# Last dense-expert stage: the product on GpSimd, the turned gates copied by VectorE

## The chip, the cores and the metric

The kernel runs on one core of one Trainium2 chip. Its time is the device time of one execution in microseconds. The core has engines with a queue each, which take their instructions in order and wait for each other by semaphores: TensorE (PE, matmuls; PEld is its loading of weights), VectorE (DVE), ScalarE (ACT), GpSimd (POOL) and SyncE (SP, which issues transfers).

## The reference

A stack of six layers works on x of 2 x 2048 x 256 values in f32, that is 4096 tokens of 256 features. The last layer, a mixture of 8 small experts of which each token uses two, is the one that the change touches:

```python
def _L1_ffn_ref(x, router_w, w1, w2, w3):
    expert_scores = x_flat @ router_w.T
    top_scores, selected = jax.lax.top_k(expert_scores, TOPK)
    top_scores = jax.nn.softmax(top_scores.astype(jnp.float32), axis=-1)
    ...
    x1 = jax.lax.ragged_dot(xb, w1b, gs)
    x3 = jax.lax.ragged_dot(xb, w3b, gs)
    h = jax.nn.silu(x1) * x3
    routed = jax.lax.ragged_dot(h, w2b, gs).astype(x.dtype)
    weighted = routed * scores_sorted[:, None]
...
x = x + 0.5 * _L0_ffn_ref(_layernorm(x, axis=-1), ...)
x = x + _L0_attn_ref(_layernorm(x, axis=-1), ...)
x = x + 0.5 * _L0_ffn_ref(_layernorm(x, axis=-1), ...)
x = x + 0.5 * _L1_ffn_ref(_layernorm(x, axis=-1), ...)
x = x + _L1_attn_ref(_layernorm(x, axis=-1), ...)
x = x + 0.5 * _L1_ffn_ref(_layernorm(x, axis=-1), ...)
```

## The kernel before

x stays in SBUF through all layers. The two `_L1_ffn_ref` layers are computed densely by `ffn1`: every token goes through all 8 experts (8 x 64 = 512 hidden features, `H1`), and a gate per token and expert, zero for six of eight, is multiplied in. `ffn1` is called twice: as ffn1a, where `combine` is given (it also sums the tables that the layer before left in HBM), and as ffn1b, the last stage of the kernel, where `combine` is None and `x_out` is given. The mixing layer (`attn1`) lies between them.

Tokens come in 8 blocks of 512 (`NB`), hidden features in 4 chunks of 128 (`NM1`, index m). For a block and chunk, TensorE makes two projections in PSUM: `ps_a` (named main_ps_k in the trace) and `ps_b` (`up`, line 2291). ScalarE writes `silu` from the one and `b16` from the other (`keep_ab`, lines 2226 and 2228). VectorE multiplies the two to `prod` (`hidden` with part 0, line 2162). The gates of a block, 16 rows of 512, are turned by TensorE into `ps_g`, copied into `gate_t`, and spread over the 128 features of chunk m by one matmul into `ps_c` (`spread`, line 2300). VectorE multiplies `prod` with `ps_c` to `h` (`hidden` with part 1, line 2167), TensorE multiplies `h` with `w2` (`down`, line 2310), and VectorE adds that to x (`add`, line 2173).

`staged` runs the blocks as a pipeline: a round has five blocks at different steps, j2 (moments of the layer norm, two rounds ahead), j1 (normalized, transposed, scored), j0 (top two and gates; its first projection), je (the experts) and jy (the output). Each engine has a function `work` that writes its part of a round; the order in it is the order of its queue. Rounds with both j2 and je are those with je from 0 to 4. In a round VectorE does the moments of j2 behind `h` of chunk 2; GpSimd computes from them the inverse deviation and shift (`ln.pool`: four small instructions, lines 309 to 316), which ScalarE uses in the next round. TensorE does, in this order: projections of chunk 1, spread 0, half of `down`, chunk 2, spread 1, transposes, chunk 3, spread 2, the other half of `down`, scores, turning of the gates, spread 3, and chunk 0 of the next block.

`ps_c` has one buffer, so the spread of chunk m + 1 waits for `h` of chunk m. `prod` has two buffers, `silu` and `b16` four each, `gate_t` one.

Of the kernel before, what the change touches and what calls it, by code (L numbers as in the profile page):

```python
# [78 lines left out]
def after(eng, sem, count):  # L79

    if not isinstance(count, int) or count > 0:
        eng.wait_ge(sem, count)
# [97 lines left out]
class Norm:  # L180
# [38 lines left out]
    def dve(self, j, tile, stored=False):  # L219

        self.dve_moments(j, tile)
        self.dve_apply(j, tile, stored)
# [1080 lines left out]
class Combine:  # L1303


    def __init__(self, nc, sc, name, x, sums, spare):
        self.nc, self.x, self.sums = nc, x, sums
        self.parts = spare[:, 0:2 * 2 * NTAB * (BT // 2) * D].bitcast(F32)\
            .rearrange("p (h n t d) -> p h n t d", h=2, n=NTAB, d=D)
        self.by_row = sums.rearrange("(n r) d -> n r d", n=NTAB)[:, 0:T].rearrange("n (q t) d -> q n t d", q=P)  # L1310
        self.waiter = sc.sb(f"{name}_waiter", [P, 1])
        self.landed = [sc.sem(f"{name}_landed{half}") for half in range(2)]
        self.added = sc.sem(f"{name}_added")
        self.first_landed = [sc.sem(f"{name}_first_landed{n}") for n in range(NTAB)]
        self.first_step = sc.sem(f"{name}_first_step")
        self.late_step = sc.sem(f"{name}_late_step")
# [12 lines left out]
    def dve_first(self, n):  # L1329
# [13 lines left out]
        v.wait_ge(self.added, 4)  # L1343
        v.memset(self.waiter[:], 0.0)

    def dve(self, j, half):

        (b, p, i), v, n, parts = j, self.nc.vector, BT // 2, self.parts
        rows = self.x[:, ds(b * BT + half * n, n), :]
        v.wait_ge(self.landed[half], 16 * b)  # L1350
        v.tensor_tensor(parts[:, half, 0:2], parts[:, half, 0:2], parts[:, half, 2:4], ALU.add)\  # L1351
            .then_inc(self.added, 1)
        v.wait_ge(self.added, 4 * b + 2 * half + 1)
        if isinstance(b, int) and b in LATE:
            count = 2 * LATE.index(b) + half + 1
            v.tensor_tensor(rows, parts[:, half, 0], rows, ALU.add).then_inc(self.late_step, 1)
            v.wait_ge(self.late_step, count)
            v.tensor_tensor(rows, parts[:, half, 1], rows, ALU.add).then_inc(self.added, 1)
        else:
            v.tensor_tensor(rows, parts[:, half, 0], parts[:, half, 1], ALU.add).then_inc(self.added, 1)  # L1360
        v.wait_ge(self.added, 4 * b + 2 * half + 2)
        v.memset(self.waiter[:], 0.0)

# [667 lines left out]
def ffn1(nc, name, x, con, ew, first, ps_a, opened, combine=None, x_out=None, load_next=None, following=None):  # L2031
# [7 lines left out]
    with Scope(nc, name) as sc:  # L2039
# [36 lines left out]
        with nc.Block() as block:  # L2076
# [14 lines left out]
            @block.gpsimd  # L2091
            def _(pool):
                opened.pool()
                each(pool, ln.pool, NB, 1 if combine else 2)
                if following:
                    following.pool_first()

            @block.vector
            def _(dve):
# [77 lines left out]

                def work(j2, j1, j0, je, jy):
                    for m in range(NM1):
                        if j0 and m == 0:  # L2180
                            gates(j0, 0)
                            gates(j0, 1)
                        if je:
                            hidden(je, m, 0)
                        if j0:
                            for n in ((2,), (3,), (4, 7, 8, 9, 10), ())[m]:
# [25 lines left out]
            def _(act):  # L2212
# [17 lines left out]
                def work(j2, j1, j0, je, jy):  # L2230
                    for m in range(NM1):
                        if m == 0:
                            if je:
                                act.wait_ge(g_turned, je[0] + 1)
                                after(act, c_made, NM1 * je[0])
                                s.activation(gate_t[:], ps_g[:, 0:BN], ACT.Copy).then_inc(g_kept, 1)
                            if j0:
                                keep_logits(j0)
# [620 lines left out]
```

## Time and profile before

| what | us |
|---|---|
| median of 3 runs | 1115.69 (1108.85 to 1122.56) |
| the profiled execution | 1114.38 |
| its span in the trace | 1112.5 |
| TensorE busy | 980.2 |
| VectorE busy | 720.9 |
| ScalarE busy | 551.0 |
| GpSimd busy | 378.6 |

The span is what the trace covers; the time of an execution has 1.88 us around it. Starts in a timeline are microseconds from the span's start. A bracket behind an instruction tells how long its engine idled before it, and for whom. The clock (PEclk) is 1.00 at 2.4 GHz and 0.50 at 1.2 GHz. The last stage takes roughly the span's last 95 us.

### The profile page before, as it was taken

The page shows a single profiled execution, that of the slowest core. Times are in us where ns is not written, and L with a number is a line of the kernel's source. Part 1 is how long each engine was busy: PE and PEld are TensorE (multiplying, and loading weights), DVE is VectorE, ACT ScalarE, POOL GpSimd, SP SyncE. Part 2 cuts the span into 40 slices and gives each one's busy share as a digit, 9 for nine tenths or more (in the row PEclk, how much of TensorE's full clock was granted, in tenths as well). Part 3 has the DMA queues.
Part 4 walks back from the last instruction along what each step waited for, and adds up shares of the span by engine and source line. Part 5 has one row for each costly group of instructions (what it writes and reads, how often), then busy time and mean ns, then how long its engine had stood idle before and what let it go on. Part 6 is the DMA issues. An engine that isn't in the chain of part 4 may idle for free. (4 is left out here: it accounts for less than half of the span.)

```text
span 1112.5 us, 17325 instructions
## 1 busy us (share of the span) xinstructions
PE 980.2 (88%) x5222; PEld 602.2 (54%) x5240; DVE 720.9 (65%) x2533; ACT 551.0 (50%) x1066; POOL 378.6 (34%) x452
## 2 busy tenths in 40 slices
PE   6999699979999799998999898956778899994886
PEld 4756566645565366665756666532334466553442
DVE  4588333137885467665688533159987699974885
ACT  6621233325666645547722333326667555534893
POOL 3106767820000223323105777801111156531110
PEclk9999799998999699999999999987889899996998
DMA  9859978864440802004246888757420000000012
GB/s 326 322 179 316 161 201 228 156 171 152 152 151 0 319 32 95 38 38 143 79 160 123 188 199 189 134 185 240 152 75 1 1 0 1 0 1 0 21 57 76
DMA packets 79656, 140.73 MB, mean 126 GB/s; under 512 B 16304, under 2 KB 47392, under 8 KB 77472
## 3 DMA queue, kind: packets, MB, share of 16 engines
q1 hardware_dynamic: 64224, 117.57, 30.8%
q0 software_dynamic: 15360, 22.29, 13.3%
q8 instruction: 33, 0.54, 0.2%
q14 instruction: 39, 0.32, 0.1%
HBM read 82.17 MB, written 58.72 MB: 127 GB/s over the span
## 5 line engine op out<-in xcount | busy, mean ns | idle before, releaser
L737 POOL DMA_INDIRECT ffn_sums<-ffn0a_xT,ffn0a_into x40 | 62.7, 1567 | 19.9 <-issue 9.3
L737 POOL DMA_INDIRECT ffn_sums<-ffn0b_xT,ffn0b_into x40 | 62.6, 1564 | 14.7 <-issue 9.5
L2291 PE MATMUL main_ps_k<-dense_first_xb,main_w 128*128 128x512 bf16 x112 | 37.8, 410 | 17.5 <-ACT ffn1a_silu L2226 8.3
L2716 PE MATMUL main_ps_k<-mixing_first_xk,mixing_wk 128*128 128x512 f32 (+1 forms) x96 | 47.0, 613 | 4.2 <-POOL main_opened_mark L1962 4.2
L1768 POOL TENSOR_TENSOR attn_attend_state_m<-attn_attend_state,attn_attend_heads 128x512 f32<-128x512 f32 x15 | 19.1, 1274 | 88.4 <-DVE attn_attend_state L1811 82.9
L2721 PE MATMUL attn_ps_r<-mixing_first_xr,mixing_wr 128*128 128x512 f32 (+1 forms) x96 | 46.2, 605 | 0.0
L1193 DVE TENSOR_TENSOR ffn0b_h<-ffn0b_sg,ffn0b_ps_b 128x160 f32<-128x160 f32 x32 | 10.3, 321 | 54.9 <-ACT ffn0b_sg L1028 54.8
L1193 DVE TENSOR_TENSOR ffn0a_h<-ffn0a_sg,ffn0a_ps_b 128x160 f32<-128x160 f32 x32 | 10.3, 321 | 54.2 <-ACT ffn0a_sg L1028 54.1
L2731 PE MATMUL attn_ps_y<-mixing_wv,attn_out 128*128 128x256 f32 (+1 forms) x192 | 43.0, 379 | 1.2 <-ACT attn_yn L2673 1.2
L866 PE MATMUL ffn0b_ps_b<-ffn0b_early,main_x 128*128 128x160 f32 x256 | 41.3, 305 | 2.6 <-DMA main_x<-w_experts 2.3
L888 PE MATMUL ffn0a_ps_b<-main_x,ffn0a_h 128*32 128x256 f32 (+2 forms) x144 | 43.5, 403 | 0.0
L888 PE MATMUL ffn0b_ps_b<-main_x,ffn0b_h 128*32 128x256 f32 (+2 forms) x144 | 43.5, 403 | 0.0
L1790 DVE COPY_PREDICATED main_spare<-attn_attend_causal,attn_attend_ps_a 128x1024 f32<-128x1024 int32 x32 | 40.0, 1302 | 4.2 <-issue 2.6
L866 PE MATMUL ffn0a_ps_b<-ffn0a_early,main_x 128*128 128x160 f32 x256 | 42.7, 312 | 0.0
L2731 PEld LDWEIGHTS attn_ps_y<-mixing_wv,attn_out 128*128 128x128 f32 (+1 forms) x192 | 36.3, 190 | 9.5 <-issue 3.3
L866 PEld LDWEIGHTS ffn0b_ps_b<-ffn0b_early,main_x 128*128 128x128 f32 x256 | 36.6, 190 | 8.1 <-DMA main_x<-w_experts 3.6
L866 PEld LDWEIGHTS ffn0a_ps_b<-ffn0a_early,main_x 128*128 128x128 f32 x256 | 37.9, 196 | 5.4 <-issue 4.2
L1351 DVE TENSOR_TENSOR main_spare<-main_spare 128x1024 f32<-128x1024 f32 x28 | 34.1, 1217 | 6.3 <-POOL main_opened_mark L1962 5.9
L2592 DVE TENSOR_TENSOR_SCAN attn_st<-mixing_keep,mixing_first_carry,attn_kr 128x512 f32<-128x512 f32 (+1 forms) x24 | 31.5, 1312 | 10.0 <-ACT attn_kr L2666 10.0
L256 POOL TENSOR_TENSOR attn_head_ln_ve<-attn_head_ln_moments,attn_head_ln_eps 128x4 f32<-128x4 f32 x8 | 2.1, 266 | 103.0 <-DVE attn_head_ln_moments L232 103.0
L1811 DVE SCALAR_TENSOR_TENSOR attn_attend_state<-attn_attend_state,attn_decay,attn_attend_ps_s 128x256 f32<-128x256 f32 x32 | 14.0, 477 | 34.2 <-PE attn_attend_ps_s L1909 34.2
L436 POOL DMA_INDIRECT ffn0a_early<-ffn_rows,ffn0a_token x10 | 12.6, 1258 | 62.0 <-issue 61.7
(498 smaller groups left out, 2682.3 us busy)
## 6 DMA issues: line engine op xcount, KB each, us to landing
main_spare<-ffn_sums SPq DMA_DIRECT2D x28, 1024.0 KB, 5.4
main_x<-w_experts SPq DMA_DIRECT2D x16, 1536.0 KB, 7.0
ffn_sums<-main_lent SPq DMA_DIRECT2D x36, 512.0 KB, 6.0
ffn_sums<-main_x SPq DMA_DIRECT2D x28, 512.0 KB, 4.1
ffn_rows<-ffn0a_early SPq DMA_DIRECT2D x8, 512.0 KB, 9.3
main_spare<-ffn_sums SPq DMA_DIRECT2D x8, 512.0 KB, 4.7
ffn_rows<-ffn0b_early SPq DMA_DIRECT2D x8, 512.0 KB, 2.9
x_out<-main_x SPq DMA_DIRECT2D x8, 512.0 KB, 2.9
```

The costliest lines, as they stand in the source:

```text
L737: g.indirect_dma_start(out=sums[:, :], out_offset=IndirectOffsetOnAxis(ap=into[:, at, j:j + 1], axis=0), in_=ys[:, n % NY, :], in_offset=N ...
L866: ins = mm(ps_b[:, p, j * CAP:(j + 1) * CAP], we[:, r, n, j, k * F:(k + 1) * F], xgT[:, k, e // ME % 2, e % ME].rearrange("p a b -> p (a b)"),
L888: ins = mm(ps_b[row:row + m, 2 + piece % 2, 0:D], eh[:, p, at:at + m], we[:, r, n, 2, :], start=True, stop=True)
L1193: v.tensor_tensor(eh[:, p, :], esg[:, p, :], ps_b[:, p, CAP:2 * CAP], ALU.mult).then_inc(eh_made, 1)
L1351: v.tensor_tensor(parts[:, half, 0:2], parts[:, half, 0:2], parts[:, half, 2:4], ALU.add)\
L1768: g.tensor_tensor(state_m[:], state[:], heads[:].unsqueeze(1).to_broadcast([P, 2, D]), ALU.mult).then_inc(s_masked, 1)
L1790: vec.copy_predicated(att[:, p, s].rearrange("p (r n) i -> p r n i", n=2), causal[:].unsqueeze(1).unsqueeze(1).to_broadcast([P, 4, 2, P]), ...
L2291: ins = mm(ps[:], wt[:, k, m * P:(m + 1) * P], xb[:, p, k, :], start=k == 0, stop=k == KD - 1)
L2592: v.tensor_tensor_scan(st[0:rows, m % 2], keep[0:rows, m:m + 1].to_broadcast([rows, BN]), kr[0:rows, m % 2], carry[0:rows, p, m:m + 1], AL ...
L2716: ins = mm(ps_k[0:rows, m % 2], wk[:, k, at:at + rows], xk[:, p, k, :], start=k == 0, stop=k == KD - 1)
L2721: ins = mm(ps_r[0:rows, m % 2], wr[:, k, at:at + rows], xr[:, p, k, :], start=k == 0, stop=k == KD - 1)
L2731: ins = mm(ps_y[:, t, :], out[0:rows, p, m, t * P:(t + 1) * P], wv[0:rows, m, :], start=m == 0, stop=m == NMH - 1)
```

## The change

In ffn1b alone, the product of `silu` and `b16` moves from VectorE to GpSimd (`products`), and the copy of the turned gates into `gate_t` from ScalarE to VectorE, where it is the first thing in a round. GpSimd's part of a round becomes `products_and_norm`: products 0, 1 and 2 of block je, then `ln.pool` of block j2, then product 3. ffn1a keeps the old division. In `Combine`, the first addition gets a function and a semaphore of its own (`paired`), and the last addition counts two, so the sums of the counts stay as they were; the same instructions run on the same engine.

```diff
+    def pairs(self, eng, j, half):
+        (b, p, i), parts = j, self.parts
+        eng.wait_ge(self.landed[half], 16 * b)
+        eng.tensor_tensor(parts[:, half, 0:2], parts[:, half, 0:2], parts[:, half, 2:4], ALU.add)\
+            .then_inc(self.paired, 1)
...
-        v.wait_ge(self.added, 4 * b + 2 * half + 1)
+        v.wait_ge(self.paired, 2 * b + half - 1)
...
             def _(pool):
                 opened.pool()
-                each(pool, ln.pool, NB, 1 if combine else 2)
+                g = nc.gpsimd
+
+                def products(j, m):
+                    b, p, i = j
+                    c = NM1 * b + m
+                    pool.wait_ge(ab_kept, c + 1)
+                    after(pool, h_made, c - 1)
+                    g.tensor_tensor(prod[:, m % 2], silu[:, m], b16[:, m], ALU.mult).then_inc(prod_made, 1)
+
+                def products_and_norm(j2, j1, j0, je, jy):
+                    for m in range(NM1):
+                        if m == 3 and j2:
+                            ln.pool(j2)
+                        if je:
+                            products(je, m)
+
+                if combine:
+                    each(pool, ln.pool, NB, 1)
+                else:
+                    staged(pool, products_and_norm, NB)
...
                 def work(j2, j1, j0, je, jy):
                     for m in range(NM1):
+                        if je and m == 0 and not combine:
+                            dve.wait_ge(g_turned, je[0] + 1)
+                            after(dve, c_made, NM1 * je[0])
+                            v.tensor_copy(gate_t[:], ps_g[:, 0:BN]).then_inc(g_kept, 1)
                         if j0 and m == 0:
                             gates(j0, 0)
                             gates(j0, 1)
-                        if je:
+                        if je and combine:
                             hidden(je, m, 0)
...
                         if m == 0:
-                            if je:
+                            if je and combine:
                                 act.wait_ge(g_turned, je[0] + 1)
                                 after(act, c_made, NM1 * je[0])
                                 s.activation(gate_t[:], ps_g[:, 0:BN], ACT.Copy).then_inc(g_kept, 1)
```

GpSimd at the start of the last stage, before (the mark that opens the stage, then the loop over the blocks with the four instructions of `ln.pool`):

```order
L1962 MEMSET main_opened_mark 128x1
L137 UNCONDITIONAL_BRANCH
L137 ISA
L309 TENSOR_TENSOR dense_ln_ve<-dense_ln_moments,dense_ln_eps 128x4
L82 REGISTER_ALU
L311 TENSOR_TENSOR dense_ln_neg_mean<-dense_ln_moments,dense_ln_minus 128x4
L82 REGISTER_ALU
L314 TENSOR_TENSOR dense_ln_rstd<-dense_ln_ve,dense_ln_power 128x4
L316 TENSOR_TENSOR dense_ln_shift<-dense_ln_neg_mean,dense_ln_rstd 128x4
```

and now, the first two rounds, which stand ahead of the loop:

```order
L1972 MEMSET main_opened_mark 128x1
L309 TENSOR_TENSOR dense_ln_ve<-dense_ln_moments,dense_ln_eps 128x4
L311 TENSOR_TENSOR dense_ln_neg_mean<-dense_ln_moments,dense_ln_minus 128x4
L314 TENSOR_TENSOR dense_ln_rstd<-dense_ln_ve,dense_ln_power 128x4
L316 TENSOR_TENSOR dense_ln_shift<-dense_ln_neg_mean,dense_ln_rstd 128x4
L2111 TENSOR_TENSOR ffn1b_prod<-ffn1b_silu,ffn1b_b 128x512 x3
L309 TENSOR_TENSOR dense_ln_ve<-dense_ln_moments,dense_ln_eps 128x4
L311 TENSOR_TENSOR dense_ln_neg_mean<-dense_ln_moments,dense_ln_minus 128x4
L314 TENSOR_TENSOR dense_ln_rstd<-dense_ln_ve,dense_ln_power 128x4
L316 TENSOR_TENSOR dense_ln_shift<-dense_ln_neg_mean,dense_ln_rstd 128x4
L2111 TENSOR_TENSOR ffn1b_prod<-ffn1b_silu,ffn1b_b 128x512
```

Three products stand ahead of `ln.pool` and one behind it; in the loop each round reads the same.

VectorE in a round of the loop, from the moments of j2 to the first step of the next round's gates (dense_ln_moments are the moments, main_x the sum into x, ffn1b_top the top scores), before:

```order
L232 BN_AGGR dense_ln_moments<-dense_ln_stats 128x2 x4
L2160 REGISTER_ALU
L2162 TENSOR_TENSOR ffn1b_prod<-ffn1b_silu,ffn1b_b 128x512
L2171 REGISTER_ALU
L2173 ISA
L2173 TENSOR_TENSOR main_x<-ffn1b_ps_y,main_x 128x512
L2167 TENSOR_TENSOR ffn1b_h<-ffn1b_prod,ffn1b_ps_c 128x512
L82 REGISTER_ALU
L2113 MEMSET ffn1b_waiter 128x1
L2115 MAX ffn1b_top<-ffn1b_logits 128x8 x4
```

and now:

```order
L232 BN_AGGR dense_ln_moments<-dense_ln_stats 128x2 x4
L2200 REGISTER_ALU
L2202 ISA
L2202 TENSOR_TENSOR main_x<-ffn1b_ps_y,main_x 128x512
L2193 REGISTER_ALU
L2196 TENSOR_TENSOR ffn1b_h<-ffn1b_prod,ffn1b_ps_c 128x512
L82 REGISTER_ALU
L2212 COPY ffn1b_gate_t<-ffn1b_ps_g 16x512
L82 REGISTER_ALU
L2142 MEMSET ffn1b_waiter 128x1
L2144 MAX ffn1b_top<-ffn1b_logits 128x8 x4
```

The product ahead of the sum into x is gone, and the copy of the gates stands between `h` of chunk 3 and the next round's gates.

## Rows read from the trace of the kernel before

**Rows 1.** Last stage by stretch: busy PE, PEld, DVE, ACT, POOL; clock; DMA.

```profile
1057.30:1067.30 10.00, 8.80 (x64) 4.62 (x65) 8.99 (x44) 9.07 (x20) 1.55 (x5) 1.00 0.16 52
...
1077.40:1087.30 9.90, 8.74 (x64) 4.72 (x66) 7.91 (x40) 9.00 (x20) 0.22 (x2) 1.00 0.25 84
```

**Rows 2.** Timeline of TensorE in the last stage: start us, length us, instruction.

```profile
1028.39 0.60 PE L2300 MATMUL ffn1b_ps_c<-ffn1b_gate_t,main_pick 16*128 16x512 bf16 x1
...
1037.53 0.39 PE L2300 MATMUL ffn1b_ps_c<-ffn1b_gate_t,main_pick 16*128 16x512 bf16 x1
...
1058.29 0.38 PE L2300 MATMUL ffn1b_ps_c<-ffn1b_gate_t,main_pick 16*128 16x512 bf16 x1
...
1062.92 0.39 PE L2300 MATMUL ffn1b_ps_c<-ffn1b_gate_t,main_pick 16*128 16x512 bf16 x1
...
1067.31 0.60 PE L2291 MATMUL main_ps_k<-dense_first_xb,main_w 128*128 128x512 bf16 x2 [0.85 <-ACT ffn1b_silu L2226]
...
1068.34 0.39 PE L2300 MATMUL ffn1b_ps_c<-ffn1b_gate_t,main_pick 16*128 16x512 bf16 x1
...
1078.37 0.38 PE L2300 MATMUL ffn1b_ps_c<-ffn1b_gate_t,main_pick 16*128 16x512 bf16 x1
```

**Rows 3.** Timeline of VectorE in the last stage, first and fourth round.

```profile
1033.37 0.69 DVE L2167 TENSOR_TENSOR ffn1b_h<-ffn1b_prod,ffn1b_ps_c 128x512 bf16<-128x512 bf16 x1
...
1062.08 0.41 DVE L2162 TENSOR_TENSOR ffn1b_prod<-ffn1b_silu,ffn1b_b 128x512 bf16<-128x512 bf16 x1
...
1062.61 0.29 DVE L2140 TENSOR_TENSOR ffn1b_hot<-ffn1b_hot,ffn1b_part 128x32 f32<-128x32 f32 x2
...
1063.49 0.68 DVE L2167 TENSOR_TENSOR ffn1b_h<-ffn1b_prod,ffn1b_ps_c 128x512 bf16<-128x512 bf16 x1
```

**Rows 4.** Timeline of GpSimd in the last stage, fourth round.

```profile
1065.98 0.29 POOL L309 TENSOR_TENSOR dense_ln_ve<-dense_ln_moments,dense_ln_eps 128x4 f32<-128x4 f32 x1 [8.36 <-DVE dense_ln_moments L232]
...
1067.51 0.20 POOL L316 TENSOR_TENSOR dense_ln_shift<-dense_ln_neg_mean,dense_ln_rstd 128x4 f32<-128x4 f32 x1
```

**Rows 5.** Timeline of ScalarE in the last stage, fourth round.

```profile
1061.36 0.59 ACT L2228 ACTIVATE ffn1b_b<-ffn1b_ps_b 128x512 bf16<-128x512 f32 x1
...
1065.48 0.59 ACT L2236 ACTIVATE ffn1b_gate_t<-ffn1b_ps_g 16x512 bf16<-16x512 bf16 x1 [0.23 <-PE ffn1b_ps_c L2300]
...
1066.50 0.20 ACT L2219 ACTIVATE ffn1b_logits<-main_ps_k 128x32 f32<-128x32 f32 x1 [0.43 <-PE main_ps_k L2274]
```

**Rows 6.** Group of the products in the last stage: busy us, mean ns.

```profile
L2162 DVE TENSOR_TENSOR ffn1b_prod<-ffn1b_silu,ffn1b_b 128x512 bf16<-128x512 bf16 x32 | 13.2, 412 | 3.0 <-ACT ffn1b_b L2228 3.0
```

**Rows 7.** Groups of GpSimd over the whole execution, shapes kept apart.

```profile
L1768 POOL TENSOR_TENSOR attn_attend_state_m<-attn_attend_state,attn_attend_heads 128x512 f32<-128x512 f32 x15 | 19.1, 1274 | 88.4 <-DVE attn_attend_state L1811 82.9 <-PE attn_attend_ps_a L1886 5.5
...
L1755 POOL TENSOR_TENSOR attn_attend_q_even<-attn_qd,main_con 128x256 f32<-128x256 f32 x32 | 18.9, 614 | 3.1 <-DVE attn_attend_heads L1825 3.1
```

**Rows 8.** Timeline of TensorE in the first dense stage.

```profile
775.31 0.58 PE L2300 MATMUL ffn1a_ps_c<-ffn1a_gate_t,main_pick 16*128 16x512 bf16 x1 [2.15 <-DVE ffn1a_h L2167]
...
782.60 0.38 PE L2300 MATMUL ffn1a_ps_c<-ffn1a_gate_t,main_pick 16*128 16x512 bf16 x1
...
789.20 0.37 PE L2300 MATMUL ffn1a_ps_c<-ffn1a_gate_t,main_pick 16*128 16x512 bf16 x1 [1.11 <-DVE ffn1a_h L2167]
```

**Rows 9.** Busy time in the first dense stage, in stretches of 1 us.

```profile
773.00:774.00 1.00, 0.16 (x1) 0.00 (x0) 0.96 (x8) 0.00 (x0) 0.00 (x0) 1.00 0.65 117
...
776.00:777.00 1.00, 1.00 (x6) 0.72 (x5) 1.00 (x6) 1.00 (x3) 0.00 (x0) 0.50 0.84 326
```

**Rows 10.** Timeline of VectorE in the first dense stage.

```profile
783.02 0.69 DVE L2167 TENSOR_TENSOR ffn1a_h<-ffn1a_prod,ffn1a_ps_c 128x512 bf16<-128x512 bf16 x1 [0.28 <-PE ffn1a_ps_c L2300]
```

**Rows 11.** Timeline of GpSimd in the mixing stage.

```profile
909.62 2.86 POOL L2551 TENSOR_TENSOR main_x<-main_x,mixing_beta 128x1024 f32 x1
```

**Rows 12.** Timeline of VectorE in the mixing stage.

```profile
908.86 1.41 DVE L2473 SCALAR_TENSOR_TENSOR mixing_first_xk<-mixing_ln_xTs,mixing_mix,mixing_first_xk 128x512 f32<-128x512 f32 x2
910.19 3.50 DVE L2473 SCALAR_TENSOR_TENSOR mixing_first_xr<-mixing_ln_xTs,mixing_mix,mixing_first_xr 128x512 f32<-128x512 f32 x2
```

More of the change, by code:

```diff
@@ L1312, in __init__ @@
         self.landed = [sc.sem(f"{name}_landed{half}") for half in range(2)]
+        self.paired = sc.sem(f"{name}_paired")
         self.added = sc.sem(f"{name}_added")
@@ L1344, in dve_first, with dve_rows @@
         v.memset(self.waiter[:], 0.0)
+    def pairs(self, eng, j, half):
[3 more added lines that the diff above has]
+            .then_inc(self.paired, 1)
     def dve(self, j, half):
+        self.pairs(self.nc.vector, j, half)
+        self.dve_rows(j, half)
+    def dve_rows(self, j, half):
         (b, p, i), v, n, parts = j, self.nc.vector, BT // 2, self.parts
         rows = self.x[:, ds(b * BT + half * n, n), :]
-        v.wait_ge(self.landed[half], 16 * b)
-        v.tensor_tensor(parts[:, half, 0:2], parts[:, half, 0:2], parts[:, half, 2:4], ALU.add)\
-            .then_inc(self.added, 1)
-        v.wait_ge(self.added, 4 * b + 2 * half + 1)
+        v.wait_ge(self.paired, 2 * b + half - 1)
         if isinstance(b, int) and b in LATE:
@@ L1357, in dve @@
             v.wait_ge(self.late_step, count)
-            v.tensor_tensor(rows, parts[:, half, 1], rows, ALU.add).then_inc(self.added, 1)
+            v.tensor_tensor(rows, parts[:, half, 1], rows, ALU.add).then_inc(self.added, 2)
         else:
-            v.tensor_tensor(rows, parts[:, half, 0], parts[:, half, 1], ALU.add).then_inc(self.added, 1)
+            v.tensor_tensor(rows, parts[:, half, 0], parts[:, half, 1], ALU.add).then_inc(self.added, 2)
         v.wait_ge(self.added, 4 * b + 2 * half + 2)
```

## Prediction

> **What bounds the kernel now.** The change touches only the last of the kernel's stages, so I read the busy time by stretch first. In a round of that stage (one block of 512 tokens, 10.0 us) TensorE is busy for 8.80 us, VectorE for 8.99, ScalarE for 9.07 and GpSimd for 1.55, at the full clock of 2.4 GHz [rows 1]. No engine is full, so the timeline of TensorE comes next. Its marker is the matmul of line 2300 that spreads the gates of chunk 0 over the features; I call it spread 0. It starts at 1037.53 and 1078.37, four rounds apart: 10.21 us a round. In the fourth round it runs from 1058.29 to 1068.34, and the longest wait of TensorE in it, 0.85 us, is for silu on ScalarE [rows 2]. ScalarE copies the turned gates at 1065.48, and then idles 0.43 us until it can read the scores at 1066.50 [rows 5]. The copy on ScalarE is followed by a wait, so it is not what ends last. VectorE starts the product of chunk 2 at 1062.08 and its h (product times spread gates) at 1063.49, just after TensorE began spread 2 at 1062.92 [rows 2, 3]. The products aren't what ends last either: the round is a loop of TensorE and ScalarE, and VectorE has some slack.
>
> **The change, part by part.**
>
> Removed: 32 products on VectorE of 412 ns [rows 6] and 8 copies of 0.59 us on ScalarE [rows 5]. Both lie beside other work in the round, as above, so by themselves they bring nothing but an earlier h of chunk 2. In before it starts 5.20 us after spread 0; without the product in front it can start when spread 2 is through, which I put at 5.0 us (4.63 to the start of spread 2, 0.39 for it) [rows 2, 3]. In the last round the products had waits beside them; I take nothing there, and one product's 0.41 us at most.
>
> Combine's new semaphore counts the same additions by the same engine: nothing.
>
> Added on GpSimd: a product of 128x512. No row shows it in bf16. The nearest is 128x512 in f32 with two inputs from SBUF, 1274 ns; the bound below is 614 ns, of 128x256, if bytes decide [rows 7]. I take 1.27, since the count of elements is the same. The Trainium skill's page GPSIMD Engine Reference (section Engine selection) speaks against the move: it gives elementwise work with two inputs to VectorE, GpSimd being about twice as slow. Here the rows make it three times (1274 against 412); with the page's two the product would take some 0.82 us (an estimate) and the sum below would lose about 1.8 us.
>
> The place of the fourth product. GpSimd does the normalization of the block that comes two rounds later ahead of product 3. This waits for VectorE's moments, which stand behind h of chunk 2. In before h of chunk 2 starts at 1063.49 and GpSimd's first step at 1065.98, 2.49 us later; its last step ends at 1067.71, after 1.73 us [rows 3, 4]. Only then comes product 3 (1.27 us), then h of chunk 3 on VectorE (0.69 us), and behind it, on the same engine, the copy of the gates that spread 0 of the next round waits for. The copy from PSUM on VectorE is in no row: ScalarE's is 0.59 [rows 5], h, which also reads PSUM, 0.69 [rows 3], the shortest thinkable that of the all-SBUF product, 0.41 [rows 6]. I take 0.60. From the start of h of chunk 2 to spread 0: 2.49 + 1.73 + 1.27 + 0.69 + 0.60 = 6.78 us. Before, it was 1068.34 - 1063.49 = 4.85. Nothing hides this: TensorE takes its queue in order, and behind spread 0 stand both halves of the output matmul, three of the four chunks and the next transposes, with h of chunk 2 at their end. So it is a closed loop: 6.78 us from h of chunk 2 to spread 0, and 5.0 us back to h of chunk 2, 11.78 us where 10.21 were.
>
> The shared port. While GpSimd's addition of 2.86 us runs from 909.62 [rows 11], two VectorE instructions with two inputs from SBUF take 3.50 us, where the same pair just before took 1.41 [rows 12]: the first waited until GpSimd was through. The Trainium skill (page SBUF — State Buffer, section SBUF: two separate sides) has this as a lock on the shared port pair, held for a whole instruction; the trace agrees (3.50 against 1.41). Here product 2 can start when ScalarE's copy of chunk 2 ends, 1061.95 in the fourth round [rows 5], and would hold until 1063.22. VectorE then stands before the gates' small multiplications, which began at 1062.61 behind a product of 0.41 that is now gone [rows 3]. They wait until 1063.22; from their start to h of chunk 2 it was 0.88 us, so h comes at 1064.10, 5.8 us after spread 0 and not 5.0. A round is then 6.78 + 5.8 = 12.58.
>
> The clock. In before TensorE waits 0.85 us in a round; now it waits some 1.9 us more in front of spread 0 (6.78 less 4.85), up to 2.7. The first dense stage shows what such waits do: after one of 2.15 us in front of its spread 0 (775.31) the granted clock went from 1.00 to 0.50, that is 1.2 GHz [rows 8, 9], and so it went after both others of about 2 us there; after 1.11 us (789.20) it did not. In the slow round spread 2 started 7.29 us after spread 0 and h of chunk 2 7.71 us after it [rows 8, 10], so such a round costs 7.71 + 6.78 = 14.49. In it the port's wait is hidden, since the matmuls are later than the gates.
>
> Five rounds have both a normalization and products (blocks 0 to 4). The first: h of chunk 2 starts at 1033.37, plus 6.78 gives 1040.15, where spread 0 of the next round stood at 1037.53 [rows 2, 3]: +2.62. The next four at full clock: 4 x (12.58 - 10.21) = +9.48. Each of these that runs at the low clock adds 14.49 - 12.58 = 1.91; I take three of the four, +5.73, since the waits lie between 1.11 and 2.15, nearer to the latter. The later rounds have no normalization, and product 3 starts at once. Sum: 2.62 + 9.48 + 5.73 = 17.8. The profiled execution took 1114.38 us, 1.3 below the median of 1115.69, so the forecast is **1132 us**, 1.5% above the median.
>
> **Rivals.** (a) The clock holds, since waits of 1.9 us fall short of what lowered it: 1114.4 + 2.62 + 9.48 = 1126.5; with no wait at the port either, 2.62 + 4 x 1.57 = 8.9, so 1123.3. For it: the new waits are slightly under the 2.15 seen; against: the port's wait lengthens them.
> (b) Clearly slower than before, over 2%: the low clock follows every one of the five waits, that of the round of block 5 too, and lasts beyond spread 2. Four low rounds give +7.64 and block 5's 7.29 - 4.63 = +2.66: 1114.4 + 12.1 + 10.3 = 1136.8. From there it is decided by the matmuls behind h of chunk 2: if these run at 1.2 GHz too, 2.9 us of work in that part (my estimate from the 8.80 busy us a round, less what lies before) doubles and overtakes the 6.78 by about 1 us in each of five rounds: 1142. For it: a wait comes in every round; against: the clock was back when spread 2 ran (0.38 us at 782.60 against 0.58 at 775.31) [rows 8].
> (c) Not slower: the round is ScalarE's (9.07 of 10.0 busy [rows 1]) and gets shorter by the copies' 0.59 in eight rounds, some 4.7 us, to 1109.7 at best. It needs spread 0 not to wait for product 3, and the order of the queues, in GpSimd and VectorE alike, says that it does; and ScalarE waits right behind the copy [rows 5]. That the executions before spread from 1108.85 to 1122.56 helps it more than the mechanism.
>
> **Chances and range.** The forecast, with two to four low rounds, 0.47; (a) 0.25; (b) 0.20; (c) 0.08. The range goes from 1119, which leaves out most of (c), to 1142, the upper end of (b): 1119 to 1142. Bounds of the unknown prices lie inside: the product at 0.61 takes 0.66 off each of five rounds (3.3), the gate copy at 0.41 another 1.0. A difference of 2% is about what a measurement of this kernel can tell from no change; slower by it means above 1138, which (b) reaches in about two thirds of its cases and the forecast with a slow set of executions: 0.19. Faster by it means below 1093, which no case gives: 0.01. Within it: 0.80.
>
> **What the profile after would show.** GpSimd's product of chunk 3 starts right after the shift step in five rounds, some 4.2 us after h of chunk 2, and h of chunk 3 on VectorE waits for GpSimd. Spread 0 waits for VectorE's copy, about 2 us in each of these rounds, and the clock reads 0.50 behind most of these waits. Rounds of 12 to 14.5 us show the loop right; rounds of 10 show it wrong. The gates' multiplications on VectorE stretch to about a microsecond where product 2 runs, if the port counts. ScalarE's busy share falls without use. The forecast fails upwards if GpSimd's bf16 product is much longer than the f32 one, and downwards if the clock holds.

## The result, and the profile after

The changed kernel takes 1132.78 us (median of 4 runs, 1126.92 to 1134.43) against 1114.68 us for the kernel before in the same series (4 runs, 1108.85 to 1122.56). The ratio is 1.0146, with a 95% interval of 1.011 to 1.0183 (the two medians divide to 1.0162): slower, by less than 2%. A second series, told below, gave 1.0154 (1.0115 to 1.0194).

The profiled execution took 1134.43 us, 20.05 more than that of before. I measure the last stage from the start of its first spread matmul to the end of the last addition into x: 93.8 us after, 79.3 before, so 14.5 us lie in it. Another 6 us lie ahead of the stage, and what follows it is 0.4 us shorter. The first spread 0 starts at 1034.36 us, before at 1028.39 [rows 2]. Over the twelve profiles of this study, whose work ahead of the stage is the same, this start lies between 1022.9 and 1034.5 (the latest is that of experiment 4, which puts 2.05 us of matmuls ahead of it); for the kernel after itself it is at 1034.4 and 1030.3, so those 6 us are no effect of the change that these runs can show. Stages and rounds are therefore compared below, and medians only for the whole.

The stage of after as one window answers to [rows 1] (stretch, length, busy us and instructions of PE, PEld, DVE, ACT, POOL, granted clock, DMA share, GB/s):

```profile
1034.36:1128.14 93.78, 72.78 (x452) 35.84 (x458) 62.59 (x254) 59.40 (x123) 43.66 (x52) 0.93 0.12 40
```

In before the same view of the stage (1028.39 to 1107.71) has TensorE busy for 67.8 us, VectorE for 64.2, ScalarE for 61.2 and GpSimd for 8.1. GpSimd is busy 35.6 us longer. VectorE gives away 32 products of 412 ns, 13.2 us, takes on 8 copies of 405 ns, 3.2 us, and yet is busy only 1.6 us less. Some 6 of the 8.4 us that are missing are in the gates' small steps, which now take longer (the one on `part` 391 ns in the mean instead of 163, the difference of the top scores 438 instead of 157). TensorE's 5.0 us more for the same 452 matmuls go with the lower clock: 0.93 over the stage, 0.97 before. The lower share alone makes some 4 us of them (an estimate from these two figures). No engine is full; the time went into waits. The timeline of TensorE after, third and fourth interval (start us, length us, and in brackets the idle time before it and for whom), answers to [rows 2]:

```profile
1059.21 0.38 PE L2333 MATMUL ffn1b_ps_c<-ffn1b_gate_t,main_pick 16*128 16x512 bf16 x1 [1.64 <-DVE ffn1b_gate_t L2212]
...
1065.16 0.39 PE L2333 MATMUL ffn1b_ps_c<-ffn1b_gate_t,main_pick 16*128 16x512 bf16 x1
...
1069.56 0.60 PE L2324 MATMUL main_ps_k<-dense_first_xb,main_w 128*128 128x512 bf16 x2 [0.87 <-ACT ffn1b_silu L2259]
...
1071.98 0.39 PE L2333 MATMUL ffn1b_ps_c<-ffn1b_gate_t,main_pick 16*128 16x512 bf16 x1 [1.33 <-DVE ffn1b_gate_t L2212]
...
1076.54 0.38 PE L2333 MATMUL ffn1b_ps_c<-ffn1b_gate_t,main_pick 16*128 16x512 bf16 x1
...
1084.21 0.60 PE L2333 MATMUL ffn1b_ps_c<-ffn1b_gate_t,main_pick 16*128 16x512 bf16 x1 [2.19 <-DVE ffn1b_gate_t L2212]
```

Spread 0 now waits for VectorE's copy of the gates, behind the old wait for silu, which is still there (0.87). The intervals are 12.77 us (1059.21 to 1071.98) and 12.23 us (to 1084.21), where they were 10.0. The other two such waits are 2.12 us (at 1046.10) and 1.73 (at 1097.28); the rounds without a normalization have none. On the clock, windows of 1 us of TensorE (length, busy us and instructions, granted clock, DMA share, GB/s), behind the wait of 1.64 us and behind that of 1.33:

```profile
1060.00:1061.00 1.00, 1.00 (x7) 0.60 0.00 0
1061.00:1062.00 1.00, 1.00 (x4) 0.50 0.00 0
1062.00:1063.00 1.00, 1.00 (x4) 0.50 0.03 8
1063.00:1064.00 1.00, 1.00 (x8) 0.69 0.00 0
1072.00:1073.00 1.00, 1.00 (x8) 1.00 0.00 0
1073.00:1074.00 1.00, 1.00 (x8) 1.00 0.00 0
```

GpSimd's timeline after, answering to [rows 4], shows the order of its queue:

```profile
1063.23 1.15 POOL L2111 TENSOR_TENSOR ffn1b_prod<-ffn1b_silu,ffn1b_b 128x512 bf16<-128x512 bf16 x1 [2.87 <-ACT ffn1b_b L2261]
...
1068.08 0.20 POOL L309 TENSOR_TENSOR dense_ln_ve<-dense_ln_moments,dense_ln_eps 128x4 f32<-128x4 f32 x1 [3.70 <-DVE dense_ln_moments L232]
...
1069.47 0.20 POOL L316 TENSOR_TENSOR dense_ln_shift<-dense_ln_neg_mean,dense_ln_rstd 128x4 f32<-128x4 f32 x1
1069.62 3.55 POOL L2111 TENSOR_TENSOR ffn1b_prod<-ffn1b_silu,ffn1b_b 128x512 bf16<-128x512 bf16 x3
1075.64 1.15 POOL L2111 TENSOR_TENSOR ffn1b_prod<-ffn1b_silu,ffn1b_b 128x512 bf16<-128x512 bf16 x1 [2.46 <-ACT ffn1b_b L2261]
```

The product at 1063.23 is product 2. Then GpSimd idles 3.70 us for the moments, with product 3 behind the normalization in its queue. At 1069.62 follow product 3 and the first two of the next block; the one at 1075.64 is that block's product 2. VectorE's timeline over the same round answers to [rows 3]:

```profile
1064.30 0.16 DVE L2165 TENSOR_SCALAR ffn1b_part<-ffn1b_part 128x8 f32<-128x8 f32 x1
...
1065.58 0.69 DVE L2196 TENSOR_TENSOR ffn1b_h<-ffn1b_prod,ffn1b_ps_c 128x512 bf16<-128x512 bf16 x1
...
1070.88 0.69 DVE L2196 TENSOR_TENSOR ffn1b_h<-ffn1b_prod,ffn1b_ps_c 128x512 bf16<-128x512 bf16 x1 [2.31 <-POOL ffn1b_prod L2111]
1071.51 0.41 DVE L2212 COPY ffn1b_gate_t<-ffn1b_ps_g 16x512 bf16<-16x512 bf16 x1
...
1075.77 1.04 DVE L2165 TENSOR_SCALAR ffn1b_part<-ffn1b_part 128x8 f32<-128x8 f32 x1
...
1077.79 0.69 DVE L2196 TENSOR_TENSOR ffn1b_h<-ffn1b_prod,ffn1b_ps_c 128x512 bf16<-128x512 bf16 x1
```

Here is the loop: h of chunk 2 at 1065.58, moments, GpSimd's normalization, product 3, h of chunk 3 at 1070.88 after a wait of 2.31, the copy, spread 0 at 1071.98: 6.40 us. And the port: the gates' step on `part` (a multiplication and an addition by constants) takes 1.04 us at 1075.77, while product 2 runs (1075.64 to 1076.79), and 0.16 at 1064.30, where product 2 (1063.23 to 1064.38) is all but over. The durations of the two new operations over the execution (ns: shortest, median, longest; first and last start):

```profile
L2111 POOL TENSOR_TENSOR ffn1b_prod<-ffn1b_silu,ffn1b_b x32: 1142/1153/1220, 1033.8 to 1122.4; 128x512 bf16<-128x512 bf16 x32
...
L2212 DVE COPY ffn1b_gate_t<-ffn1b_ps_g x8: 405/405/413, 1030.5 to 1116.4; 16x512 bf16<-16x512 bf16 x8
```

### The profile page after: what moved, and what is told of

Its sections match the earlier page's. It is cut to its first block and busy times, and to the rows that moved or that the text cites. A ratio compares the mean times of both kernels' runs of the same rounds, so it can differ in the third digit from the quotient of the medians.

```text
span 1132.6 us, 17351 instructions
## 1 busy us (share of the span) xinstructions
PE 992.4 (88%) x5222; PEld 606.8 (54%) x5240; DVE 719.5 (64%) x2509; ACT 547.8 (48%) x1058; POOL 416.3 (37%) x484
## 5 line engine op out<-in xcount | busy, mean ns | idle before, releaser
L2324 PE MATMUL main_ps_k<-dense_first_xb,main_w 128*128 128x512 bf16 x112 | 41.1, 441 | 16.0 <-ACT ffn1b_silu L2259 7.0
L1778 POOL TENSOR_TENSOR attn_attend_state_m<-attn_attend_state,attn_attend_heads 128x512 f32<-128x512 f32 x15 | 19.1, 1274 | 87.1 <-DVE attn_attend_state L1821 81.6
L2111 POOL TENSOR_TENSOR ffn1b_prod<-ffn1b_silu,ffn1b_b 128x512 bf16<-128x512 bf16 x32 | 36.8, 1156 | 32.1 <-ACT ffn1b_b L2261 30.1
L1193 DVE TENSOR_TENSOR ffn0b_h<-ffn0b_sg,ffn0b_ps_b 128x160 f32<-128x160 f32 x32 | 10.3, 321 | 54.4 <-ACT ffn0b_sg L1028 54.2
L1193 DVE TENSOR_TENSOR ffn0a_h<-ffn0a_sg,ffn0a_ps_b 128x160 f32<-128x160 f32 x32 | 10.3, 321 | 53.6 <-ACT ffn0a_sg L1028 53.4
L2196 DVE TENSOR_TENSOR ffn1b_h<-ffn1b_prod,ffn1b_ps_c 128x512 bf16<-128x512 bf16 x32 | 21.9, 685 | 26.6 <-POOL ffn1b_prod L2111 16.2
```

The source lines that it names most:

```text
L2111: g.tensor_tensor(prod[:, m % 2], silu[:, m], b16[:, m], ALU.mult).then_inc(prod_made, 1)
L2196: v.tensor_tensor(h[:, p, m], prod[:, q], ps_c[:], ALU.mult).then_inc(h_made, 1)
L2324: ins = mm(ps[:], wt[:, k, m * P:(m + 1) * P], xb[:, p, k, :], start=k == 0, stop=k == KD - 1)
```

## The experiments

The theory has three parts: the order on GpSimd (normalization ahead of product 3) makes the loop; the clock falls behind the waits that the loop makes; and product 2 on the shared port holds up the gates. The rivals are that VectorE is the bound, since the copy of the gates stands in its queue, or that GpSimd's products are too slow in whatever order. "Rounds" are the distances from one spread 0 to the next; the stage is measured as above. Each ratio is to runs of the kernel before in the same series.

| kernel | rounds (us) | stage (us) | ratio to before (95%) |
|---|---|---|---|
| before | 9.14, 10.73, 10.03, 10.05, 10.03, 9.91, 8.66 | 79.3 | |
| after | 11.74, 13.11, 12.77, 12.23, 13.07, 11.35, 9.40 | 93.8 | 1.0146 (1.011 to 1.0183) |
| after, once more | 11.57, 12.80, 12.17, 13.13, 13.08, 11.30, 10.56 | 94.7 | 1.0154 (1.0115 to 1.0194) |
| 1: normalization behind product 3 | 9.50, 10.70, 10.73, 10.69, 10.63, 10.56, 10.58 | 83.5 | 1.0025 (1.0005 to 1.0044) |
| 2: gates copied by ScalarE again | 11.46, 12.57, 12.06, 12.89, 11.99, 9.94, 9.39 | 90.4 | 1.0159 (1.0121 to 1.0197) |
| 3: only the copy of the gates moved | 9.08, 10.78, 10.06, 10.09, 9.98, 9.95, 8.66 | 79.7 | 1.0001 (0.9977 to 1.0024) |
| 4: matmuls in the wait | 10.56, 12.26, 12.15, 12.23, 12.11, 9.76, 9.39 | 88.6 | 1.0100 (1.0027 to 1.0174) |
| 5: 1, with silu ahead of the scores | 9.02, 11.07, 10.70, 10.73, 10.70, 10.20, 9.40 | 81.9 | 0.9997 (0.9976 to 1.0018) |
| 6: 1, with product 2 on VectorE | 9.11, 10.70, 10.23, 10.21, 10.15, 10.07, 9.62 | 80.2 | 0.9983 (0.9954 to 1.0012) |
| 7: 6, with silu ahead of the scores | 8.13, 10.71, 10.22, 10.23, 10.16, 10.06, 10.35 | 80.8 | 0.9996 (0.9970 to 1.0021) |
| 8: before, with silu ahead of the scores | 8.84, 10.45, 10.03, 9.99, 10.01, 9.91, 8.67 | 78.2 | 0.9956 (0.9935 to 0.9977) |
| 8, once more | 8.40, 10.45, 10.03, 9.98, 10.01, 9.90, 8.66 | 77.7 | 0.9975 (0.9950 to 0.9999) |

### 1. The order on GpSimd

```diff
                 def products_and_norm(j2, j1, j0, je, jy):
                     for m in range(NM1):
-                        if m == 3 and j2:
-                            ln.pool(j2)
                         if je:
                             products(je, m)
+                        if m == 3 and j2:
+                            ln.pool(j2)
```

> The changed kernel with one exchange in GpSimd's queue: in a round, product 3 comes ahead of the normalization of the block two rounds later. Everything else is as in the changed kernel (products on GpSimd, gate copy on VectorE). I measure the last stage by the trace, from the start of the first spread matmul to the end of the last addition into x: 79.3 us before the change, 93.8 after. Theory (the loop: moments, normalization, product 3, h of chunk 3, gate copy, spread 0): it is cut, rounds are 10.0 to 10.4 us again, the stage 79 to 82 us, the time 1113 to 1119. Rival (GpSimd's longer product, 1.15 against 0.41 us, and its hold on the shared port cost the time wherever they stand): rounds stay above 11.5 us, the stage at 88 or more, the time above 1125.

Measured: 10.3 us of the 14.5 are gone with two lines exchanged; rounds of 10.7, no wait of TensorE for the copy, clock 1.00 in the rounds with a normalization. The order made the loop. But rounds (10.0 to 10.4) and stage (79 to 82) of the theory are missed: the result lies between the two cases, far nearer to the theory. Some 1.2 us of the stage come from the last interval, where the clock fell to 0.50 (10.58 us against 9.40 in experiment 5). For the rest, the timelines show where the rounds stop short of before's 10.0: GpSimd's product 2 at 1059.72, then VectorE at the gates, then TensorE's spread 0 on either side of them.

```profile
1059.72 1.15 POOL L2111 TENSOR_TENSOR ffn1b_prod<-ffn1b_silu,ffn1b_b 128x512 bf16<-128x512 bf16 x1 [0.97 <-ACT ffn1b_b L2261]
```

```profile
1060.06 0.84 DVE L2165 TENSOR_SCALAR ffn1b_part<-ffn1b_part 128x8 f32<-128x8 f32 x1
...
1061.88 0.69 DVE L2196 TENSOR_TENSOR ffn1b_h<-ffn1b_prod,ffn1b_ps_c 128x512 bf16<-128x512 bf16 x1
```

```profile
1055.35 0.39 PE L2333 MATMUL ffn1b_ps_c<-ffn1b_gate_t,main_pick 16*128 16x512 bf16 x1
...
1066.04 0.39 PE L2333 MATMUL ffn1b_ps_c<-ffn1b_gate_t,main_pick 16*128 16x512 bf16 x1
```

The multiplication starts behind product 2 and ends when that ends (0.84 us, at 1060.9), and h of chunk 2 comes 6.53 us after spread 0, where before it came 5.20. It doesn't wait for product 2 itself, which is ready at 1060.87, before spread 2 is through (1060.62 and 0.39). Product 1 does the same to an earlier step of the gates: a pair of comparisons (line 2159) that took 0.29 us in before takes 1.24 at 1057.55.

### 2. The gates copied by ScalarE again

```diff
-                        if je and m == 0 and not combine:
-                            dve.wait_ge(g_turned, je[0] + 1)
-                            after(dve, c_made, NM1 * je[0])
-                            v.tensor_copy(gate_t[:], ps_g[:, 0:BN]).then_inc(g_kept, 1)
...
-                            if je and combine:
+                            if je:
                                 act.wait_ge(g_turned, je[0] + 1)
```

> The changed kernel with the gate copy back on ScalarE; products on GpSimd with the normalization ahead of product 3. Theory (the loop): spread 0 no longer waits for product 3, but half of the output matmul right behind it still needs h of chunk 3, so a round loses only the copy and the spread, some 0.7 us; five rounds, 3.5 us: the stage 90 to 91 us, the time 1126 to 1130. Rival (the place of the gate copy behind h of chunk 3 is the cause): the stage returns to 80 to 82 us, the time to 1114 to 1118.

Measured: a stage of 90.4 us, as the theory has it. The median of 1131.76 us isn't, and its ratio is no lower than that of the kernel after: four runs, from 1125.65 (the profiled one) to 1133.93, don't show the 3.4 us, so the reading rests on the rounds. The loop stays without the copy in it: the rounds at full clock take 11.99 to 12.06 us where they took 12.23. The rest of the 3.4 us comes from the clock, which stays up in one round more and in that of block 5. Spread 0 now waits for h of chunk 3 itself, since `ps_c` has one buffer. Here are two of the rounds, with the windows behind the waits (columns: PE, PEld, DVE, ACT, POOL, clock, DMA share, GB/s):

```profile
1052.95 0.37 PE L2329 MATMUL ffn1b_ps_c<-ffn1b_gate_t,main_pick 16*128 16x512 bf16 x1 [1.15 <-DVE ffn1b_h L2196]
1065.01 0.57 PE L2329 MATMUL ffn1b_ps_c<-ffn1b_gate_t,main_pick 16*128 16x512 bf16 x1 [1.60 <-DVE ffn1b_h L2196]
```

```profile
1053.00:1057.00 4.00, 3.48 (x23) 2.14 (x24) 3.54 (x20) 2.45 (x7) 1.27 (x2) 1.00 0.04 15
1065.00:1069.00 4.00, 3.99 (x14) 1.80 (x14) 2.22 (x18) 2.08 (x7) 1.34 (x2) 0.57 0.00 0
```

In the interval of 12.06 that begins at 1052.95 the clock is 1.00; that of 12.89 from 1065.01 begins at 0.57.

### 3. Only the copy of the gates moved

The kernel before, with the copy on VectorE and the products left on VectorE (Combine's new semaphore stays in, so the run shows that it costs nothing either):

```diff
+                        if je and m == 0 and not combine:
+                            dve.wait_ge(g_turned, je[0] + 1)
+                            after(dve, c_made, NM1 * je[0])
+                            v.tensor_copy(gate_t[:], ps_g[:, 0:BN]).then_inc(g_kept, 1)
...
-                            if je:
+                            if je and combine:
                                 act.wait_ge(g_turned, je[0] + 1)
```

> Of the change only the gate copy on VectorE; products stay on VectorE, GpSimd does the normalization alone. Theory (the loop needs product 3 behind the normalization): VectorE ends h of chunk 3 about 1 us before spread 0 is due, the copy of 0.41 us fits in: the stage 79 to 80 us, the time as before, 1112 to 1118. Rival (VectorE, 9.0 of 10.0 us busy, is the bound once the copy comes on top): 0.35 us in each of eight rounds, the stage 82 to 83 us, the time some 1118.

Measured: 79.7 us, ratio 1.0001. VectorE can take the copy at no cost, even with all four products; the rival that makes VectorE the bound falls. ScalarE gains nothing either, as the waits of ScalarE from 1037 to 1077 show (us in all, times, longest):

```profile
ACT ffn1b_logits L2249 <- PE main_ps_k L2304: 4.2, 4, 1.2
```

In before these four waits came to 1.8 us, the one of [rows 5] to 0.43. The 2.4 us more are the four copies of 0.59: the copy's time went into the wait behind it.

### 4. Matmuls in the wait

```diff
                         up(je, 1)
+                        if not combine and j2:
+                            for _ in range(12):
+                                mm(ps_r[:, P:512], w1[:, 0, 0:P], xb[:, je[1], 0, 0:384], start=True, stop=True)
                         spread(je, 0)
```

> The changed kernel with 12 matmuls of 384 columns into an unused part of the scores' bank ahead of spread 0 in the rounds with a normalization, about 1.9 us of work where TensorE waited 1.3 to 2.2 us; their results are not used. Theory (the waits let the clock fall, and the slow matmuls lengthen the loop): the granted clock stays at 1.00, rounds are 12.1 to 12.4 us instead of 12.2 to 13.1, the round of block 5 10.0 instead of 11.35, the stage 90 to 91 us, the time 1127 to 1131. Rival (the clock's fall is covered by other waits): rounds and stage as after the change, 93.5 to 95 us, the time 1131 to 1135.

The added matmuls write to a part of a PSUM buffer that nothing reads. Measured: the clock holds, in TensorE's timeline, in a window of ten us over it, and over the whole stage (the last line has TensorE alone):

```profile
1067.13 2.11 PE L2355 MATMUL main_ps_k<-dense_first_xb,main_w 128*128 128x384 bf16 x12
1069.44 0.39 PE L2333 MATMUL ffn1b_ps_c<-ffn1b_gate_t,main_pick 16*128 16x512 bf16 x1 [0.20 <-DVE ffn1b_gate_t L2212]
```

```profile
1066.00:1076.00 10.00, 9.48 (x71) 5.33 (x71) 6.99 (x32) 7.70 (x16) 5.58 (x6) 1.00 0.15 52
...
1034.47:1123.04 88.57, 74.12 (x500) 1.00 0.13 42
```

The rounds are 12.1 to 12.3 with the clock at 1.00, as the one round of the kernel after that kept it (12.23), so 12.2 is the loop and what is above it the clock. From the second to the fifth interval that is 51.18 - 48.75 = 2.43 us, in that of block 5 another 1.59: some 4.0 us. The stage of 88.6 flatters this kernel, since the matmuls ahead of the first spread 0 (2.05 us) lie outside the measure; with them it is 90.6, 3.2 below the kernel after. The median is 3.4 below (1129.42), but with four runs each the intervals overlap, so the rounds carry the argument. One thing doesn't fit a price per wait: no matmuls were added ahead of spread 0 of block 5, TensorE waits 2.18 us there (at 1093.78), and the clock holds all the same. So the wait in front of a round doesn't by itself bring the clock down; what else decides it these runs leave open.

### 5 and 7. Silu ahead of the scores, with the products on GpSimd

Experiment 5 is 1 with this on ScalarE; 7 is 6 with it:

```diff
                     s.activation(silu[:, m], ps_a[:], ACT.Silu).then_inc(a_kept, 1)
+                    if scored:
+                        keep_logits(scored)
                     act.wait_ge(b_made, c + 1)
...
-                            if j0:
+                            if j0 and (combine or not je):
                                 keep_logits(j0)
                         if je:
-                            keep_ab(je, m)
+                            keep_ab(je, m, j0 if m == 0 and not combine else None)
```

> The kernel with the exchange in GpSimd's queue (product 3 ahead of the normalization), whose last stage took 83.5 us in rounds of 10.7, with one more exchange: ScalarE makes silu of chunk 0 ahead of its copy of the scores. Theory (what is left over is the port: product 2 on GpSimd holds up the gates on VectorE, so moments, normalization and the block two rounds ahead come later): the exchange moves nothing that these wait for, rounds 10.4 to 10.7 us, stage 81.5 to 83.5. Rival (the rounds are those of TensorE waiting 0.85 us for silu of chunk 0): 0.5 us less in each of seven rounds, stage 79.5 to 80.5.

Measured: 81.9 us; the inner rounds are 10.70 with it and without it, and what is gained is in the first and the last two, 1.2 of the 1.6 us in the last, where this time the clock held (9.40 instead of 10.58). So silu isn't what keeps 1 at 10.7.

> As the one with product 2 back on VectorE, and ScalarE makes silu of chunk 0 ahead of its copy of the scores. Theory: with loop and port away the rounds are bound by TensorE and ScalarE again, whose wait of 0.85 us for silu of chunk 0 shrinks to some 0.3: rounds 9.5 to 9.8 us, stage 76 to 77.5, time 1110 to 1113, below the kernel before. Rival (VectorE or the normalization bounds the rounds at 10 us): stage 79.5 to 80.5, the time as before.

Measured: 80.8 us and rounds of 10.2, like those of 6. The theory that silu sets what is left fails: TensorE's wait for silu of 0.86 us fell to 0.43, and no inner round got shorter. (The first interval is 1.0 us shorter, the last 0.7 longer, with the clock at 0.50 in it.) What waits in two rounds of 7 (1045 to 1067) is VectorE for GpSimd's product of chunk 1, and ScalarE for the shift:

```profile
DVE ffn1b_h L2206 <- POOL ffn1b_prod L2120: 2.5, 2, 1.4
```

```profile
ACT dense_ln_xn L2001 <- POOL dense_ln_shift L316: 2.3, 3, 0.8
```

### 6. The product next to the gates back on VectorE

Experiment 1, with product 2 on VectorE (its semaphore is a second one):

```diff
-                        if m == 3 and j2:
-                            ln.pool(j2)
-                        if je:
+                        if je and m != 2:
                             products(je, m)
+                        if m == 3 and j2:
+                            ln.pool(j2)
...
-                        if je and combine:
+                        if je and (combine or m == 2):
                             hidden(je, m, 0)
```

> The kernel with the exchange in GpSimd's queue, and product 2 back on VectorE; products 0, 1 and 3 stay on GpSimd, the gate copy on VectorE. Theory (the port): nothing on GpSimd runs beside the gates' later steps, the step on part takes 0.17 us instead of 0.84 to 1.04, h of chunk 2 comes some 5.2 us after spread 0 instead of 5.84, rounds are 10.0 to 10.2 us instead of 10.7, the stage 79.5 to 80.5 us, the time 1113 to 1117. Rival (the product's length on GpSimd, whichever chunk, makes the 0.65 us): rounds stay at 10.5 or more, stage 82.5 to 83.5.

Measured: 80.2 us, rounds of 10.15 to 10.23; h of chunk 2 comes 5.56 us after spread 0 (1060.22), later than the 5.2 expected. In VectorE's timeline the later steps of the gates are undisturbed, while an earlier one, beside product 0 (1059.98 to 1061.13), still takes 0.70 us instead of 0.16:

```profile
1060.46 0.70 DVE L2163 TENSOR_TENSOR ffn1b_diff<-ffn1b_top 128x4 f32<-128x4 f32 x1
...
1064.36 0.42 DVE L2200 TENSOR_TENSOR ffn1b_prod<-ffn1b_silu,ffn1b_b 128x512 bf16<-128x512 bf16 x1
1064.70 0.17 DVE L2174 TENSOR_SCALAR ffn1b_part<-ffn1b_part 128x8 f32<-128x8 f32 x1
...
1065.78 0.68 DVE L2206 TENSOR_TENSOR ffn1b_h<-ffn1b_prod,ffn1b_ps_c 128x512 bf16<-128x512 bf16 x1
```

An operation of 0.42 us put back into VectorE's queue shortens the round by half a microsecond, since it replaces one of 1.15 on the other engine that shut VectorE out. So the round doesn't pay for a product of 1.15 us as such (three of them are still there), but for product 2 beside the gates' later steps. The kernel before isn't beaten by it (0.9983, 0.9954 to 1.0012).

### 8. Silu ahead of the scores in the kernel before

The edit of 5, in the kernel before.

> The kernel before the change with one exchange in its last stage: ScalarE makes silu of chunk 0 ahead of its copy of the scores. Theory (rounds before the change are a loop of TensorE and ScalarE): the 0.85 us wait of TensorE shrinks to 0.2 to 0.4, rounds 9.5 to 9.7 us instead of 10.05, stage 76 to 77.5 instead of 79.3, time 2 to 3 us below the kernel before. Rival (VectorE, 9.0 us busy in 10, bounds them): rounds 9.9 to 10.1, stage 79 to 80.

Measured: the stage is 1.1 us shorter, but in its first intervals; the inner rounds stay at 10.0 although the wait of 0.85 us [rows 2] is cut into pieces. TensorE's waits for silu from 1037 to 1087 (us in all, times, longest; in before 3.8, 5, 0.9), and VectorE's from 1037 to 1077:

```profile
PE main_ps_k L2293 <- ACT ffn1b_silu L2226: 2.1, 9, 0.3
```

```profile
DVE ffn1b_prod L2162 <- ACT ffn1b_b L2230: 1.5, 4, 0.4
```

So the longest wait of TensorE was not what set the round. What does, these runs leave open: VectorE and ScalarE are each busy for 9.0 of 10.0 us, with short waits for each other and for TensorE. It isn't the busy time of either alone: experiment 3 gave VectorE 0.41 us a round more and ScalarE 0.59 less, and the rounds stayed. The median, 0.9956, is better than 1.1 us of 1114 explain (0.1%), hence a second series, together with the kernel after:

> The kernel before, with silu of chunk 0 ahead of the logits on ScalarE in the last dense stage, once more. Its stage was 78.2 us against 79.3 us, its median 0.9956 of the kernel before. If only the stage's 1.1 us is real, the ratio comes out at 0.997 to 1.001; if the rest of the 5 us is real too, at 0.994 to 0.997, with the first spread matmul of the stage at 1024 us or earlier again.

> The changed kernel as it stands, once more. Its last dense stage (first spread matmul to the last addition into x) took 93.8 us in the first profile, with rounds of 11.4 to 13.1 us, and the first spread matmul came at 1034.4 us, 6.0 us later than in the kernel before. If the stage is the whole effect of the change, the stage comes out at 92.5 to 95 us again, and the first spread matmul anywhere between 1022 and 1035 us, since the starts in ten profiles of the same code ahead of it lie there. If the change also delays what runs ahead of the stage, that matmul comes at 1032 us or later again.

Measured: 8 has 0.9975 (0.9950 to 0.9999), with a stage of 77.7 and its first spread 0 at 1025.2. The ratio and the first spread 0 (not 1024 or earlier) fit the case in which only the stage's gain is real. The interval covers the other case too, so the edit is worth 1 to 2 us in the stage, and whether more stays open. It is the only version below the kernel before that was run in two series, and it stood below in both. The kernel after has a stage of 94.7 us with the first spread 0 at 1030.3: the stage repeats, the late start didn't, as the case expected in which the stage is the whole effect.

## Why the prediction was right, and where its sizes were off

The forecast was 1132, the median is 1132.78. The mechanism and its place are shown by experiments 1, 4 and 6. That the number agrees to 1 us is luck: the terms sum to 17.8 us, all in the stage, while the stage grew by 14.5 and 15.4 in two profiles and the medians by 18.1 and 16.6.

- **What bounded the kernel.** "A loop of TensorE and ScalarE", with the wait for silu as its sign, was wrong: experiment 8 took that wait apart and the round stayed. It did no harm to the sum, since the new loop is longer than whatever set the old one. The copy and the products as work beside other work: right for the copy (3). In 1, 5, 6 and 7 fewer products on VectorE bring no shorter round.
- **The product on GpSimd**, taken as 1.27 from an f32 row [rows 7]: 1.15. The Trainium skill (page GPSIMD Engine Reference, section Engine selection) gives about twice VectorE's time. The measurement is 1153 against 412 ns [rows 6], 2.8 times. The prediction's side estimate for a product of 0.82 us, a sum lower by 1.8, counts four rounds; five have the product, which makes 0.45 x 5 = 2.25. **The copy on VectorE**, taken as 0.60: 0.41. From h of chunk 2 to spread 0 it took 6.40 and 6.42 us instead of 6.78. From start to start the shown round has 2.50 to the normalization, 1.54 to product 3, 1.26 to h of chunk 3, 0.63 to the copy and 0.47 to spread 0, where 2.49, 1.73, 1.27, 0.69 and 0.60 were taken: the steps of the normalization, of h and of the copy were put too long, and the shorter product brought nothing, since h of chunk 3 starts 0.1 us after its end.
- **The port.** Spread 0 to h of chunk 2 was put at 5.8 us with the port; it was 5.81 (1071.98 to 1077.79). The instruction that waited was not the pair of [rows 3] but the step on `part` ahead of it. A round at full clock: 12.23 where 12.58 was expected; four of them cost 8.1 instead of 9.48.
- **The clock, the step that was mis-sized.** Three of the four rounds at 1.2 GHz came as predicted, behind waits of 2.12, 1.64 and 2.19 us. But a low round was put at 14.49, from the first dense stage, and took 12.77 to 13.11: spread 2 came 5.95 us after spread 0 (1059.21 to 1065.16), not 7.29, since here the clock read 1.00 again from 1064.2, 5.0 us after spread 0, and in the first dense stage only from 782, 6.7 us after it. The four rounds together cost 10.34, not 15.21, in both profiles of the kernel after. The prediction's reading of that stage also left out a case: behind a wait of 1.28 us (at 854.70) the clock fell to 0.50 at 857.
- **The first interval**: +2.60 (+2.43 in the second profile), predicted +2.62. Two errors cancel in it: h of chunk 2 came 5.38 us after spread 0 (1039.74) instead of 4.98, and spread 0 came 6.36 after that instead of 6.78.
- **What the sum left out.** The interval of block 5 grew by 1.44, of which experiment 4 gives the clock the whole; it stood in rival (b) only, as 2.66. The last interval grew by 0.74, and what follows it shrank by 0.66. Sum: 2.60 + 10.34 + 1.44 + 0.74 - 0.66 = 14.46.
- **The rivals.** (a), the clock holds: out, though experiment 4 shows what it would have been like, some 4 us less. (b): the low clock did reach block 5, but not the matmuls behind spread 2, so the 2% weren't passed. (c): out; where only the copy moves (3), the rounds don't shorten.

## What to carry to other kernels

When work moves to an idle engine, look at what it is queued behind there: here two lines in another order were worth 10 of 14.5 us, and three of the four products on GpSimd, in the right order and away from the gates' later steps, cost less than 1 us of the stage and gained nothing. A wait on TensorE has a second price, the lower clock behind it, which is read from a stretch of the same kernel, but its length there need not carry over, and not every such wait is followed by it. The longest wait of the busiest engine isn't by itself the bound: take it away in a run before a sum is built on it.

## What the hardware showed that was not expected

- VectorE's stall beside a GpSimd product hits small instructions with one input too, and lasts until the product ends: a TENSOR_SCALAR of 128x8 in f32 took 1.04 us instead of 0.16. The rows of before showed it only for instructions with two inputs [rows 12]. The Trainium skill (page SBUF — State Buffer, section SBUF: two separate sides) names VectorE's two-port modes beside two SBUF inputs for this lock; the rows agree if this instruction runs in such a mode, which they don't show.
- GpSimd's time follows the elements far more than the bytes: 128x512 took 1153 ns in bf16 and 1274 in f32, half the elements in f32 614 [rows 7].
- The copy of 16x512 from PSUM takes 405 ns on VectorE and 590 on ScalarE [rows 5].
- The length of a single wait of TensorE doesn't tell whether the clock falls. Behind waits of 1.33 us (after), 1.15 and 1.43 us (experiment 2) the clock read 1.00; behind the four of 1.64 to 2.19 us in after it fell to 0.50, and behind the two of 1.60 and 1.91 us in experiment 2 it read 0.57 and 0.65 over 4 us. But behind 1.76 us in experiment 2 (at 1089.89) and 2.18 us in experiment 4 (at 1093.78) it read 1.00, and in the last intervals of experiments 1 and 7 it fell to 0.50 where no wait was over 1.01 and 1.24 us. What decides it stays open.
